# Cross attention: keys loaded as 14 column parts instead of seven, values as four pieces instead of one

## What is computed

```python
def _L1_xattn_ref(q, k, v, Wq, bq, Wo, bo):      # q: normed x; k = v = ctx_1024, 12544 rows
    qp = (q @ Wq.T + bq).reshape(b, l, H, E)
    kp = (k @ Wq.T + bq).reshape(b, s, H, E)
    vp = (v @ Wq.T + bq).reshape(b, s, H, E)
    scale = 1.0 / np.sqrt(E)
    scores = jnp.einsum('blhe,bshe->bhls', qp, kp)
    attn = jax.nn.softmax(scale * scores, axis=-1)
    out = jnp.einsum('bhls,bshd->blhd', attn, vp)
    return out @ Wo.T + bo
```

## Time and profile before

| | |
|---|---|
| median of three runs | 911.43 us |
| the profiled execution | 904.64 us |
| its span, first to last instruction | 902.9 us |
| first key load issued | 480.35 us |
| first maximum of the cross attention | 514.7 us |
| last key load issued | 765.9 us |
| last maximum of the cross attention | 793.8 us |
| mean granted TensorE clock | 0.911 |

### The profile page before, as it was taken

How to read it: one execution, slowest core, us unless ns; L and a number is a source line. 1 busy time by engine, 2 the same in 40 slices (tenths; PEclk the granted TensorE clock), 3 DMA queues, 4 the chain that set the end, 5 groups by cost and what they waited for, 6 DMA issues and landing times. The chain is left out here.

```text
span 902.9 us, 20452 instructions
## 1 busy us (share of the span) xinstructions
PE 800.6 (89%) x8176; PEld 631.7 (70%) x8176; DVE 619.7 (69%) x1158; ACT 538.4 (60%) x920; POOL 123.5 (14%) x130
## 2 busy tenths in 40 slices
PE   5999999989999998886789677999999999997655
PEld 5888878878878676576469435777777777776344
DVE  5656767878878888872244496899989989920231
ACT  3777786787887877853152003677677767776100
POOL 2232222222222333021030000000000000000010
PEclk9999999999999999898699655999999999999556
DMA  3466546626653632099969992899989988251000
GB/s 126 147 161 182 155 133 155 183 85 187 171 148 116 137 61 71 22 182 239 367 142 167 216 214 73 132 205 160 212 199 167 218 202 147 90 216 28 6 1 6
DMA packets 101310, 131.47 MB, mean 146 GB/s; under 512 B 25752, under 2 KB 91674, under 8 KB 100444
## 3 DMA queue, kind: packets, MB, share of 16 engines
q1 hardware_dynamic: 101216, 130.17, 60.5%
HBM read 90.43 MB, written 39.70 MB: 144 GB/s over the span
## 5 line engine op out<-in xcount | busy, mean ns | idle before, releaser
L1935 DVE TENSOR_REDUCE unit_max<-bank 128x1 f32<-128x512 f32 (+1 forms) x350 | 221.4, 675 | 27.9 <-PE bank L1087 26.5
L1457 ACT ACTIVATE prob<-bank 128x1024 f32<-128x1024 f32 (+1 forms) x200 | 191.0, 1004 | 78.8 <-PE bank L1111 78.0
L728 PE MATMUL bank<-hc_high,w_high 128*128 128x256 f32 x392 | 117.7, 300 | 7.5 <-DVE w_low L1597 4.7
L1087 PE MATMUL bank<-k_stack,q_max 49*128 49x512 f32 (+1 forms) x400 | 106.6, 538 | 11.8 <-DVE unit_max L1931 6.8
L1111 PEld LDWEIGHTS bank<-q_stack,k_stack 49*128 49x128 f32 x1568 | 106.2, 194 | 12.5 <-issue 3.7
L728 PE MATMUL bank<-hc_low,w_high 128*128 128x256 f32 x392 | 111.7, 285 | 0.0
L728 PE MATMUL bank<-hc_high,w_low 128*128 128x256 f32 x392 | 111.7, 285 | 0.0
L1126 PE MATMUL bank<-prob,vals 128*32 128x128 f32 x3136 | 111.4, 285 | 0.0
L1111 PE MATMUL bank<-q_stack,k_stack 49*128 49x128 f32 x1568 | 106.1, 274 | 3.0 <-ACT prob L1457 0.9
L1640 DVE SCALAR_TENSOR_TENSOR normed<-bank,b_centered,rstd_wide 128x256 f32<-128x256 f32 x196 | 85.4, 477 | 28.5 <-ACT rstd_wide L1284 28.5
L1277 ACT ACTIVATE square<-bank,b_centered 128x256 f32<-128x256 f32 x196 | 81.9, 471 | 34.0 <-PE bank L728 34.0
(11 more groups left out here) (311 smaller groups left out, 1180.6 us busy)
## 6 DMA issues: line engine op xcount, KB each, us to landing
k_stack<-k_scratch SPq DMA_DIRECT2D x336, 112.0 KB, 5.7
vals<-v_scratch SPq DMA_DIRECT2D x8, 1666.0 KB, 8.1
hc_raw<-in_ctx_t SPq DMA_DIRECT2D x49, 256.0 KB, 3.1
v_scratch<-vst SPq DMA_DIRECT2D x9, 1088.0 KB, 9.7
k_scratch<-k_high SPq DMA_DIRECT2D x37, 256.0 KB, 3.4
k_scratch<-k_low SPq DMA_DIRECT2D x37, 256.0 KB, 3.5
w_ffn<-in_l SPq DMA_DIRECT2D x4, 1920.0 KB, 17.9
w_l<-in_l SPq DMA_DIRECT2D x6, 603.0 KB, 6.0
```

The lines of the kernel that those rows point to most:

```text
L728: last = nc.tensor.matmul(out_ap, lhs, rhs, start=(n == 0), stop=(n == len(pairs) - 1))
L1087: last = nc.tensor.matmul(bank[:, at, 0:hi - lo], q_max[head_rows[hh], s, :], k_stack[s % 2][head_rows[hh], lo:hi], start=True, stop=True)
L1457: A(prob[:, e % NPB, :, 0:width], bank[:, at:at + 2, 0:width], ACT.Exp).then_inc(c_exp, 1)
L1935: V.tensor_reduce(unit_max[:, s % 2, u, hh:hh + 1], bank[:, at[hh], 0:width], AX_X, ALU.max, negate=True).then_inc(c_red, 1)
```

## The change

The column part `CHUNK` goes from 1792 to 896 columns, so that a row in a key DMA is 3584 B instead of 7168 B, and there are 14 parts to a pair instead of seven, each with its own semaphore, its own wait for `c_sc` on SP and its own wait for `c_stack` on TensorE. The values of a pair are loaded in four DMAs (three of 425 columns, one of 391, that is 1700 and 1564 B a row) instead of one of 6664 B a row, and `weigh` waits for all four. No byte more or less is moved, and nothing is computed differently.

```diff
-CHUNK = 1792
+CHUNK = 896
 CHUNKS = S // CHUNK
+V_PARTS = 4
+PIECE_COLS = -(-TILES // V_PARTS) * VW
@@ load_values
                 if s >= 2:
                     sp.wait_ge(c_wt, EU * (s - 1))
-                sp.dma_start(vals[:, s % 2, :, 0:TILES * VW],
-                             v_scratch[2 * s:2 * s + 2].rearrange("h p c -> p h c")).then_inc(c_vals[s % 2], 16)
+                for q in range(V_PARTS):
+                    cols = slice(q * PIECE_COLS, min((q + 1) * PIECE_COLS, TILES * VW))
+                    sp.dma_start(vals[:, s % 2, :, cols],
+                                 v_scratch[2 * s:2 * s + 2, :, cols].rearrange("h p c -> p h c")).then_inc(c_vals[s % 2], 16)
@@ weigh
                 if u == 0:
-                    pe.wait_ge(c_vals[s % 2], 16 * (s // 2 + 1))
+                    pe.wait_ge(c_vals[s % 2], 16 * V_PARTS * (s // 2 + 1))
```

## The result

The changed kernel takes 967.06 us in the median of four runs (960.31 to 976.30), against 913.41 us for four runs of the kernel before. Some executions of any kernel here fall into a slower state of the chip, and the ratios with an interval leave these out (here 976.30 us). So taken, the ratio is 1.0574, with a 95% interval of 1.0485 to 1.0662. The profiled execution took 960.31 us, 55.7 us more than the one before (904.64 us).

A forecast was written before the change was run, and what follows sets the result against it. SP's issuing of loads becomes the bound: keys 311.1, values 13.7, fills 0.66, fetches 35 and 1.5 make 362 us; with 2.7 us to landing the end moves 51.2 us, giving 955.8 to 962.6, taken as 960 us, range 932 to 985.

The forecast's parts named there:

- No DMA wait to remove: Cross attention: loads are already hidden by SP's waits and a 27.9 us lead, so finer loads remove no TensorE wait.
- Price of an issue, 0.463 us whatever the bytes: Key DMAs on SP: each costs 0.463 us, going with rows or engines served, not bytes; bounds 0.345 and 0.51 us.
- SP's path of 362 us, last key issue at 842.3 us: SP from first key DMA at 480.35 us to pair 7's last: keys, values, fills and fetches together 362 us.
- Fetches, 35 x 1.0 us: SP from 521 us on: 35 instruction fetches each hold its next issue 1.0 us, 35 us; bounds 0.7 and 1.3.
- 2.7 us from the last issue to the last maximum: End of the key loads: last key lands 2.7 us after its issue, at 845.0 us, taken as the last maximum's start.
- TensorE waiting for keys in nearly every part from pair 3 on: Cross attention: lead of some 20 us at pair 1 is gone in pair 3; TensorE then waits some 50 us in all.
- 41.7 us a pair: below SP's 45.9, so no cost while SP sets the pace: Cross attention at a lower granted clock: engines at 1.67 us a unit still outpace SP, so no time is added.
- three quarters: Sign in the cross attention: TensorE's busy share would fall to near three quarters, with a lower granted clock.
- A: Rival: SP's issues still fit, at or below 0.387 us each, so not slower, 905 to 912 us; chance 0.07.
- B: Rival: instruction fetches do not add to SP's issue time; end shifts 16 us, 924 us; chance 0.08.
- C: Rival: the transfers become the bound, at 0.53 us a piece 20 us more, 980 us; chance 0.08.
- D: Rival: low clock over the last 34 us costs at most 7 us, 967 us; chance 0.10.

The follow-up runs named there:

- parts11: Changed kernel with key parts of 1152 columns, 11 parts and 66 key DMAs a pair, values still in four pieces; 913.77 us, ratio 1.0021.
- values_only: Changed kernel with keys back in seven parts of 1792 columns, values still in four pieces; runs of 908.82, 909.72, 930.98 and 938.71 us.
- uneven: Kernel before, with each of the six key DMAs of a part split into 1728 and 64 columns; 962.20 us, ratio 1.0554.
- parts16: Changed kernel with key parts of 784 columns, 16 parts and 96 key DMAs a pair; 1010.73 us, ratio 1.1087.
- pool_fetch: Changed kernel with 4032 one-element memsets added on idle GpSimd, to cause more instruction fetches; 991.50 us in one execution.
- half_weigh: Changed kernel with half of the weighing's matmuls left out, SP's program and all bytes the same; 1000.54 us in one execution.
- pool_low: Changed kernel with 28 of the 84 key DMAs a pair issued by GpSimd instead of SP from pair 2 on; 908.72 us, ratio 0.9976.
- keys_only: Changed kernel with values in one DMA as before, keys still in 14 parts; 966.65 us, ratio 1.0636.

## Why the prediction was right, step by step

The forecast was 960 us and a shift of 51.2 us; measured were 967 us and, between the profiled executions, 55.7 us. The mechanism is the one named.

- **No DMA wait to remove:** right. parts11 has shorter rows and leaves the time; so does values_only, as far as its two short runs tell.
- **Price of an issue, 0.463 us whatever the bytes:** right, from 256 B to 7 KB a row (uneven), and by the slope of parts16. Four value pieces cost 1.96 us where 1.95 was taken.
- **SP's path of 362 us, last key issue at 842.3 us:** 363.0 us and 842.9 us. SP's waits were to vanish nearly, and they did: no pause of it is a wait for TensorE. So the sum is not right by luck, each of its terms is met.
- **Fetches, 35 x 1.0 us:** right in number and size for the 16 KB packets of TensorE's program. The reading that any fetch does it was never written as a term, but pool_fetch shows that it would have been wrong: 8 KB packets of another engine cost next to nothing.
- **2.7 us from the last issue to the last maximum:** this term was mis-sized, it is 6.3 us, and that is most of the 4.2 us that the sum missed on the profile. TensorE at that place:

```profile
845.03 0.70 PE L1091 MATMUL bank<-k_stack,q_max 49*128 49x512 f32 x2 [2.40 <-DMA k_stack<-k_scratch]
845.67 1.94 PE L1130 MATMUL bank<-prob,vals 128*32 128x128 f32 x32
847.53 0.79 PE L1091 MATMUL bank<-k_stack,q_max 49*128 49x512 f32 x2
848.13 1.22 PE L1115 MATMUL bank<-q_stack,k_stack 49*128 49x128 f32 x16
849.19 0.33 PE L1091 MATMUL bank<-k_stack,q_max 49*128 49x256 f32 x2
```

The last piece landed 2.1 us after its issue, and TensorE, which had waited 2.40 us for it, began at once. But the last part's 896 columns are needed by three units, and TensorE's fixed order puts weighing and scores between their maxima. The prediction took the last maximum to start when the last part lands.
- **TensorE waiting for keys in nearly every part from pair 3 on:** wrong, it waits 11 times from 549 to 845 us.
- **Clock, "41.7 us a pair: below SP's 45.9, so no cost while SP sets the pace":** the 41.7 us are wrong. I took the pace of the stretch at 0.74 for that of half clock. These are two stretches of the kernel after:

```profile
584.00:619.00 35.00, 34.41 (x658) 26.91 (x656) 32.26 (x53) 25.41 (x29) 0.00 (x0) 1.00 0.51 147
...
653.00:688.00 35.00, 34.57 (x408) 27.11 (x408) 20.29 (x33) 15.89 (x19) 0.00 (x0) 0.55 0.54 154
```

At 0.55, TensorE is busy 34.6 of 35 us and 33 reductions are done, 16.5 units: 2.1 us a unit, 53 us a pair, more than SP's 46. Where the clock is low TensorE falls behind SP, and where it returns it catches up and waits. The page shows it in sum: the same 8176 matmuls are busy 843.2 us instead of 800.6. That is also, I take it, why TensorE's busy share stayed at 88% where I foretold three quarters, and why its waits for keys are 16.3 us by name and not 50: much of what would have been waiting is slower work (42.6 us more of it). That this cost nothing while SP set the pace still held in the kernel after, by luck rather than by my number: SP never had to pause, and TensorE was waiting for the last keys when they came. It did not hold in half_weigh, where SP paused for 10.2 us. Otherwise the price of the low clock is behind the last key issue, in the lag of the last maximum and in the last scores, and there it differs from execution to execution.

Of the rivals, A is refuted by the 420 ns, B by the 35 held issues. C is refuted by pool_low and by the 2.1 us to landing. D, the low clock over the last 34 us, did not happen in the profiled execution (0.89 and 0.99 there) but did in part in keys_only and wholly in pool_fetch, and pool_fetch's 13 us are more than the 7 us that I gave as its most.

The rule that the time to start a DMA is usually small relative to the DMA itself (the Trainium skill, "DMA: Bandwidth & Descriptors", section "Issuing engines are not separate DMA queues") does not hold for this size: 0.463 us to issue against 0.34 us of transfer. What the same sentence of it says, that issuing from several engines saves only the sequencer's time, is what pool_low shows to be worth 58 us (966.65 or 967.06 less 908.72 us).

No version beats the kernel before: pool_low and parts11 stand with it, and nothing shows that values_only does not. Their pace is still that of TensorE and VectorE, 34.8 us a pair, and TensorE hardly waits for a load (1.2 us in parts11, nothing in the other two).

## What to carry to other kernels

Before splitting loads, multiply: DMAs per period times the spacing of issues on their queue (0.463 us here), plus what instruction fetches take, must stay below the period of the engines that use the data. Up to that point a split costs nothing and brings nothing where no engine waits for a load. Beyond it the queue first uses up its lead, which hides the loss in a short loop (parts11: 39.0 us a pair against 34.8, and no loss over eight pairs); from then on every further DMA costs its full issue time. If short pieces are wanted, divide them between queues. And look at the granted clock where an engine is said to be the bound: in half_weigh TensorE had fewer matmuls, stayed at half clock and became the slower one.

## What the runs showed of the hardware

- SP's issue of a 16-row DMA takes 420 ns behind another, from 256 B to 6.9 KB a row; 302 ns after a pause. GpSimd's takes 484 ns (pool_low).
- A 16 KB packet of TensorE's instructions holds SP's next issue by about 1.0 us (35 of 36). 8 KB packets for GpSimd's program, 31 more of them, add 2 us in all (one execution). What makes the difference is open: size, queue and engine were not told apart.
- The granted clock stayed at 1.2 GHz for over 350 us in half_weigh (515 to 890 us), with TensorE busy 364.3 of these 375 us. Leaving out work made that kernel slower than the changed one, 1000.54 against 972.42 us, as one execution shows.
- A wait that the profile lists need not be a pause: all 9.5 us listed for SP in the kernel after belong to issues that began 44 or 45 ns behind the end of the one before, which is the usual gap.
